# Restack from two queues, later staged splits, regrouped token work and later query parts in a two-layer cross-attention kernel

## The chip, the cores and the metric

The kernel runs on one core of a Trainium2 chip. The metric is the device time of one execution in microseconds (us), lower is better. The engines are PE (matrix multiply; PEld is its weight load), DVE (vector), ACT (scalar), POOL (GpSimd) and SP (which here only issues transfers). Each engine works through its own list of instructions in order and waits on semaphores.

## The reference

Two layers over queries x (8 batches of 64 rows, width 256) and a context of 8 x 1601 rows:

```
x = x + cross_attention_0(layernorm(x), ctx)      # 16 heads of width 16
x = x + head_attention(layernorm(x))
x = x + top1_expert_ffn(layernorm(x))             # 8 experts
x = x + cross_attention_1(layernorm(x), ctx)
x = x + state_space(layernorm(x))                 # 64-step scan, gelu, layer norm
x = x + top2_moe(layernorm(x))                    # router, gate/up/down with 8 experts
```

Everything is float32. The kernel writes many operands as two float16 parts, a high part and a low part, and makes three products of them (high x high, high x low, low x high).

## The kernel before

**Rounds and steps.** The two cross-attentions are 16 rounds `g` (8 batches in layer 0, then 8 in layer 1). The 1601 context rows are 13 row tiles, so each round has 13 steps `k`. `STEP_UNITS` writes out by hand what each step holds: `S` scores and their exponentials on ACT, `W` the weighted sum over values, `K`/`N` key projections of a later round in four quarters times two halves, `V` value projections, `P` score maxima (PE makes them, DVE reduces them into `mpart`), `T` and `O` the row constants and the division. A key unit K is made by PE, evacuated twice by ACT (`k32` at L1093, `kh` at L1094), and its low part `kl` is made by POOL (L643).

**Restacking.** `restack(r, mt)` on SP (L497) waits for the low parts of four key units and then issues 12 transfers that copy `kh` and `kl` into `ks`, the layout that the scores read. In round `g` SP does `restack(g + 1, 0)` in step 1 and `restack(g + 1, 1)` in step 8. Within a step SP's order is: restack, `load_high_queries`, context loads, and then the events of the step. Two things wait for `stacked0`: the scores of the round, and ACT's evacuation of the next round's first key units (L1088), since `kh` is reused. Before round 0 there is a prologue written out in `PROLOGUE_UNITS`.

**Events.** `MID` and `SSM` place the other work in the steps: key `n` of `MID` for token tile `t` falls on step 13 x (2t + 2) + 6 + n, counted from the start of round 0. The queries of layer 1 are made by `q_make` (PE, ACT), `q_parts`, `q_mask` and `q_store` (DVE), and SP's `store_queries` writes them to memory with three transfers that raise `q_out` by 48. Key 27 of tile t is step 7 of round 2t + 4. The head attention of tile t + 1 begins in the same round: its `a_v` falls on step 9, and DVE there waits for all earlier stores:

```
dve.wait_ge(sem("a_v_mm"), t + 1)
dve.wait_ge(sem("q_out"), 48 * (TT + t))
nc.vector.tensor_copy(a_v[:, :], mid[:, 0:D]).then_inc(sem("a_v"), 1)
```

PE's `a_qk` in step 10 writes the bank that this copy reads, so it waits for `a_v`. `STAGE_AT` places the splits of six staged weights (ACT makes the high part, DVE the low part), and SP loads a next one after each.

**The tail.** After round 15 `TAIL` lists by hand: `g` and `d` are parts of the gate product on PE; `x` scales and transposes tokens of one expert (POOL or ACT scales, PE transposes, ACT takes the high part) and `y` takes the low part on DVE; `h` and `l` are the high and low split of an expert weight tile (ACT, then DVE). `transpose_tokens(i)` waits for the low part of token group i - 2. Groups 26 to 39 stand among 32 `d` parts.

Of the kernel before, what the change touches and what calls it, by code (L numbers as in the profile page):

```python
# [13 lines left out]
P = 128  # L14
# [13 lines left out]
E = 8  # L28
# [25 lines left out]
PROLOGUE_UNITS = ("Q K0 K1 P0 P1 K2 P2 K3 P3 V0 P4 P5 K4 P6 P7 K5 P8 K6 P9 V1 P10 K7 P11 N0 P12 N1 P13 N2 P14 P15 "  # L54
                  "T N3").split()
FIRST_CTX_HIGH = {"K1": 4, "K3": 5, "V0": 6, "K4": 7}
FIRST_CTX_LOW = {"P2": 4, "P4": 5, "P6": 6, "P7": 7}
STEP_UNITS = {0: ["V2", "S", "P0", "W"],
              1: ["V3", "S", "P1", "W"],
# [23 lines left out]
MID = {0: ["out"], 1: ["a_norm"], 2: ["a_turn"], 3: ["a_v"], 4: ["a_qk"], 5: ["a_e"], 6: ["a_p"], 7: ["a_w"],  # L83
       8: ["a_z"], 9: ["a_x"], 10: ["f_norm"], 13: ["f_turn"], 14: ["f_gate"], 15: ["f_pick"], 16: ["f_0"],
       17: ["f_1"], 18: ["f_2"], 19: ["f_3"], 20: ["f_end"], 21: ["q_norm"], 22: ["q_turn"], 23: ["q_make"],
       24: ["q_parts"], 26: ["q_mask"], 27: ["q_store"]}

SSM = {0: ["out"], 1: ["s_norm"], 2: ["s_turn"], 3: ["s_u"], 4: ["s_0"], 5: ["s_1"], 6: ["s_2"], 7: ["s_3"],
       8: ["s_4"], 9: ["s_5"], 10: ["s_y"], 13: ["g_stats"], 14: ["g_norm"], 16: ["g_parts"], 17: ["g_clean"],
       18: ["m_stats"], 20: ["m_norm"], 21: ["m_turn"], 23: ["r_logits"], 27: ["r_pick"]}  # L90
SSM_THIRD = {0: ["out"], 1: ["s_norm"], 2: ["s_turn"], 3: ["s_u"], 4: ["s_0"], 5: ["s_1"], 6: ["s_2"], 7: ["s_3"],
             8: ["s_4"], 9: ["s_5"], 10: ["s_y"], 11: ["g_stats"], 12: ["g_norm"], 13: ["g_parts", "g_clean"],
             14: ["m_stats"], 15: ["m_norm"], 16: ["m_turn"], 17: ["r_logits"], 18: ["r_pick"]}
QUERIES = ["q_stats", "q_norm", "q_turn", "q_make", "q_parts", "q_mask", "q_store"]
FIRST = {(0, 0): 1, (1, 4): 2, (1, 9): 3}
STAGE_JOBS = 7
STAGE_AT = {(0, 2): 1, (0, 6): 2, (0, 8): 3, (0, 10): 4, (0, 12): 5, (1, 1): 6}
POWERS_AT = {(0, 7): 0, (0, 9): 1, (0, 11): 2, (0, 12): 3, (1, 0): 4}
SPLIT_AT = {(G - 1, 8): 0, (G - 1, 11): 1}

# [17 lines left out]
for e in range(E):  # L118
    TAIL += ["g"] * min(2, len(GATE_PARTS) - TAIL.count("g")) + [f"x{X_THIRD + e}", f"y{X_THIRD + e}"]
TAIL += ["g"] * (len(GATE_PARTS) - TAIL.count("g"))  # L120
for n in range(len(LAST_GATE_PARTS)):
    TAIL.append("d")
    if n % 2 and 0 <= (n - 3) // 2 < len(X) - X_BOTH:
        TAIL += [f"x{X_BOTH + (n - 3) // 2}", f"y{X_BOTH + (n - 3) // 2}"]
    if n % E == E - 1:
        TAIL += [f"h{GATES + n // E}", f"l{GATES + n // E}"]

UNITS = [(0, it) for it in range(GATES)] + [(1, it) for it in range(GATES)] + \
        [(r, it) for it in range(GATES, IT) for r in range(2)]
# [142 lines left out]
def build(nc, d, out):  # L272
    with ExitStack() as ctx:
# [10 lines left out]
        def need(eng, name, value):  # L284

            if value > 0:
                eng.wait_ge(sem(name), value)
# [179 lines left out]
        def _(sp):  # L467
# [29 lines left out]
            def restack(r, mt):  # L497

                sp.wait_ge(sem("klo_done"), K_UNITS * r + 4 * mt + 4)
                need(sp, "main_mm", 2 * KT * (r - 1) if r > 1 else 0)  # L500
                for j in range(4):
                    for n, part in enumerate((kh, kl, kh)):
                        load(ks[r % 2][n + 1:P:PARTS, 4 * mt + j, :], part[32 * j:32 * j + 32, mt, :], f"stacked{mt}")

# [125 lines left out]
        @block.gpsimd  # L630
        def _(pool):
            def load(dst, src, name):
                pool.dma_start(dst, src).then_inc(sem(name), 16)

            def inverse_root(i):

                pool.wait_ge(sem("var_ready"), i + 1)
                nc.gpsimd.tensor_tensor(rstd[:, :], ve[:, :], half[:, :], ALU.pow).then_inc(sem("rstd_ready"), 1)

            def klo(r, ku):  # L640
                mt, (k0, w) = ku // 4, QUARTERS[ku % 4]
                pool.wait_ge(sem("khi_done"), K_UNITS * r + ku + 1)
                nc.gpsimd.tensor_tensor(kl[:, mt, k0:k0 + w], k32[:, ku % 2, 0:w], kh[:, mt, k0:k0 + w],  # L643
                                        ALU.subtract).then_inc(sem("klo_done"), 1)

            def scale_tokens(i):

                r, e, t0, t1 = X[i]
                if i == 0:
                    pool.wait_ge(sem("k_mm"), K_UNITS * B)  # L650
                    pool.wait_ge(sem("v_mm"), V_UNITS * B)
                pool.wait_ge(sem("cmb_done"), t1)
                need(pool, "xcT_mm", i - 1)
                for t in range(t0, t1):
                    ins = nc.gpsimd.tensor_scalar(xg[:, i % 2, t - t0, :], xm[:, t, :], cmb[:, TT * r + t, e:e + 1], None,
                                                  ALU.mult)
                ins.then_inc(sem(f"xg_ready{i % 2}"), 1)

            def event(name, layer, t):
                if name == "r_pick" and t in (1, TT - 1):  # L660
                    for i in range(2):
                        scale_tokens((0 if t == 1 else X_THIRD) + i)
                elif name == "x":
                    if t + 2 < len(X) and t + 2 not in (X_THIRD, X_THIRD + 1) and not scaled_by_act(t + 2):
                        scale_tokens(t + 2)
                elif name == "q_stats":
                    inverse_root(t)
                elif name in ("out", "a_x", "f_end", "g_stats", "m_stats"):
                    to = {"out": "s_" if layer else "a_", "a_x": "f_", "f_end": "q_", "g_stats": "g_",
                          "m_stats": "m_"}[name]  # L670
                    inverse_root(stats_index(to, 1, t))

            nc.gpsimd.memset(half[:, :], -0.5).then_inc(sem("half_ready"), 1)
            nc.gpsimd.memset(qcur[0][:, :, :], 0.0)
            nc.gpsimd.memset(qcur[1][:, :, :], 0.0).then_inc(sem("qcur_zero"), 1)
            load(small[:, :], d["small"], "const_in")
            load(bias[:, :, :], d["bias"], "const_in")
            load(rows[:, :, :], d["rows"][:, 0:4, :], "const_in")
            load(sel[:, :], d["sel"], "const_in")
            load(fb32[:, :], d["fb"], "const_in")  # L680
            load(wo[:, :, :], d["wo"][0], "wo0_in")
            load(am[:, 0, :, :], d["am"], "am_in")
            load(bT[:, :, :], d["bT"], "ssm_in")
            load(cT[:, :], d["cT"], "ssm_in")
            load(rw[:, :, :, :], d["rw"], "rw_in")
            load(rdw[:, :, :], d["rdw"], "rw_in")
            pool.wait_ge(sem("half_ready"), 1)
            inverse_root(0)
            nc.gpsimd.memset(v[:, :, :, DH:VW], 1.0).then_inc(sem("v_ones"), 1)
            for ku in range(8):  # L690
                klo(0, ku)
            for ku in range(4):
                klo(1, ku)
            for g in range(G):
                for k in range(KT):
                    for name in STEP_UNITS[k]:
                        if name[0] in "KN" and has_unit(name, g):
                            klo(round_of(name, g), int(name[1]))
                    for name, layer, t in events(g, k):
                        event(name, layer, t)  # L700
            for item in TAIL:
                if item[0] == "x":
                    event("x", 1, int(item[1:]))
                else:
                    event(item, 1, TT - 1)
            for it in range(IT):
                pool.wait_ge(sem("ihi_done"), it + 1)
                nc.gpsimd.tensor_tensor(il[:, it, :], i32[:, it % 2, :], ih[:, it, :],
                                        ALU.subtract).then_inc(sem("ilo_done"), 1)
# [343 lines left out]
        def _(act):  # L1053
            def split_stage(z):
# [11 lines left out]
                    ins = nc.scalar.activation(fbp[:, 0, :], fb32[:, :], ACT.Copy, scale=W_SCALE)  # L1066
                ins.then_inc(sem("stage_hi"), 1)

            def split_ctx(n):
                g, i, s = n // 4, n % 4, ctx_slot(n)  # L1070
                h, kc, u = i // 2, i % 2, g % 2
                k0, w = HALVES[h]
                act.wait_ge(sem(f"ctx_in{s}"), 16 * ctx_loads(n))

                need(act, "v_mm", V_UNITS * (g - 2) + (4 if h == 0 else V_UNITS))
                need(act, f"parts_stored{u}", 32 * (g // 2))
                nc.scalar.activation(ch[u][:, kc, k0:k0 + w], c32[s][:, 0:w], ACT.Copy).then_inc(sem("chi_done"), 1)  # L1077
# [78 lines left out]
            def event(name, layer, t):  # L1156
# [8 lines left out]
                elif name == "q_make":  # L1165
# [3 lines left out]
                    for mt in range(2):  # L1169
# [3 lines left out]
                        else:  # L1173
                            ins = nc.scalar.activation(q32[:, mt, :], o, ACT.Copy)
                    ins.then_inc(sem("q32_done"), 1)
                elif name == "stage":
                    split_stage(t)
                elif name == "power":
# [58 lines left out]
            for name in PROLOGUE_UNITS:  # L1237
                if name != "Q":
                    after_unit(name, int(name[0] == "N"), True)
                if name in FIRST_CTX_HIGH:  # L1240
                    split_ctx(FIRST_CTX_HIGH[name])
            act.wait_ge(sem("const_in"), 80)
            for g in range(G):
                for k in range(KT):
# [42 lines left out]
        def _(dve):  # L1287
# [143 lines left out]
            def event(name, layer, t):  # L1431
# [72 lines left out]
                    stats(xt)  # L1504
                elif name == "q_parts":
                    q = TT * layer + t
                    dve.wait_ge(sem("q32_done"), q + 1)
                    need(dve, "q_out", 48 * q)
                    link(nc.vector.tensor_copy(qh[:, :, :], q32[:, :, :]))
                    link(nc.vector.tensor_tensor(ql[:, :, :], q32[:, :, :], qh[:, :, :], ALU.subtract))  # L1510
                elif name in ("q_mask", "q_store"):
                    two = range(2) if name == "q_mask" else range(2, 4)
# [205 lines left out]
```

## Time and profile before

| what | value |
|---|---|
| runs, median (lowest to highest) | 1031.73 us (1030.37 to 1033.67), 3 runs |
| the profiled execution | 1028.6 us, span 1026.8 us |
| mean granted clock of PE | 0.990 of full speed |
| PE, DVE, ACT, POOL busy | 92%, 60%, 53%, 20% |
| prologue before the first scores | 0 to 49.26 us |
| 16 rounds | 49.26 to about 735 us |
| tail and expert products | from about 735 us to the end |

Rows of a timeline read: start, duration, engine and line, operation, tiles, count; in square brackets the idle time of the engine just before it and what ended it. SPq is SP issuing a transfer. A waiting row of PE is time lost only where PE sets the end.

### The profile page before, as it was taken

What the parts mean: (1) busy time and instruction counts of PE and PEld (TensorE: products, weight loads), DVE (VectorE), ACT (ScalarE), POOL (GpSimd) and SP (SyncE); (2) the same over time, 40 slices, a digit from 0 to 9 for tenths busy, and PEclk for the clock granted to TensorE, in tenths of its full rate; (3) what the DMA queues carried; (4) which work ended last, traced back from release to release, by engine and by line L of the source; (5) the groups of instructions that cost most, each with busy time, mean ns of one, the idle gap of its engine ahead of it and who ended that gap; (6) DMA issues with size and microseconds to landing.
All of it is one profiled execution on the core that took longest, in us unless ns stands there. A gap on an engine that the chain in (4) does not pass through costs nothing.

```text
span 1026.8 us, 35579 instructions
## 1 busy us (share of the span) xinstructions
PE 947.6 (92%) x15476; PEld 625.1 (61%) x15476; DVE 620.9 (60%) x1046; ACT 545.0 (53%) x1032; POOL 201.2 (20%) x233
## 2 busy tenths in 40 slices
PE   4789889999999999999999999997898899999998
PEld 2356566656656665666666656656687544445887
DVE  5665665667485565857667776775764574445332
ACT  4467766776677667456666666656625421212200
POOL 4211112111111212111121121232446100000000
PEclk9999999999999999999999999999999999999999
DMA  8587375452735352454334444423221322232100
GB/s 301 137 313 231 87 253 133 143 169 73 209 92 156 107 129 70 116 133 122 93 113 119 107 120 119 103 56 126 85 83 41 124 101 104 82 107 99 42 1 22
DMA packets 70829, 123.79 MB, mean 121 GB/s; under 512 B 34770, under 2 KB 46082, under 8 KB 67412
## 3 DMA queue, kind: packets, MB, share of 16 engines
q1 hardware_dynamic: 69812, 119.84, 39.4%
q8 instruction: 124, 2.03, 0.8%
q0 software_dynamic: 576, 1.35, 0.4%
q10 hardware_dynamic: 288, 0.33, 0.1%
q14 instruction: 29, 0.24, 0.1%
HBM read 64.81 MB, written 17.32 MB: 80 GB/s over the span
## 4 chain that ended last, share of the span: by engine, by line
PE 72%; DVE 11%; ACT 7%; issue 4%; DMA 2%; SPq 2%; POOL 1%; ACTq 0%; DVEq 0%; POOLq 0%
PE ps L714 70%; DVE mpart L1354 3%; ACT p L1119 3%; SPq L469 2%; DVE rinv L1371 1%; DMA c32a<-in_ctxT 1%; ACT ch L1077 1%; DMA c32b<-in_ctxT 1%; PE ps L853 1%; DVE cl L1329 1%; ACT kh L1094 1%; DVE wl L1385 1%; ACT k L1093 1%; PE ps L883 1%; ACT wh L1134 1%
## 5 line engine op out<-in xcount | busy, mean ns | idle before, releaser
L1354 DVE TENSOR_REDUCE mpart<-ps 128x2 f32<-128x800 f32 (+1 forms) x256 | 252.5, 988 | 136.0 <-PE ps L714 135.1
L1119 ACT ACTIVATE p<-ps 128x512 f32<-128x512 f32 (+1 forms) x416 | 225.6, 595 | 186.2 <-PE ps L714 184.8
L643 POOL TENSOR_TENSOR kl<-k,kh 128x400 f16<-128x400 f32 (+1 forms) x128 | 117.6, 920 | 458.4 <-ACT kh L1094 458.4
L714 PE MATMUL ps<-p,v 128*17 128x64 f32 x6656 | 131.8, 222 | 1.6 <-issue 1.6
L714 PEld LDWEIGHTS ps<-p,v 128*17 128x17 f32 x6656 | 98.1, 98 | 39.8 <-issue 37.3
L714 PE MATMUL ps<-wvh,ch 128*128 128x256 f16 (+1 forms) x416 | 114.3, 275 | 1.9 <-issue 1.9
L714 PE MATMUL ps<-xch,wh 128*128 128x512 f16 (+2 forms) x384 | 114.3, 312 | 0.0
L714 PE MATMUL ps<-xcl,wh 128*128 128x512 f16 (+2 forms) x384 | 114.2, 311 | 0.0
L714 PE MATMUL ps<-xch,wl 128*128 128x512 f16 (+2 forms) x384 | 114.0, 311 | 0.0
L714 PE MATMUL ps<-wvl,ch 128*128 128x256 f16 (+1 forms) x416 | 113.5, 273 | 0.0
L714 PE MATMUL ps<-wvh,cl 128*128 128x256 f16 (+1 forms) x416 | 113.4, 273 | 0.0
L714 PE MATMUL ps<-kh,qbcur 64*128 64x400 f16 (+1 forms) x512 | 86.8, 336 | 25.4 <-DVE mpart L1354 22.1
L1385 DVE SCALAR_TENSOR_TENSOR wl<-w,wh 128x2048 f16<-128x2048 f32 x24 | 55.0, 2291 | 82.9 <-ACT wh L1134 82.9
L714 PEld LDWEIGHTS ps<-qcur,ks 64*128 64x128 f16 (+1 forms) x3328 | 61.3, 97 | 65.5 <-issue 51.3
L714 PE MATMUL ps<-qcur,ks 64*128 64x64 f16 (+1 forms) x3328 | 85.7, 192 | 10.5 <-ACT p L1119 6.1
L714 PE MATMUL ps<-ch,wkh 128*128 128x400 f16 (+1 forms) x256 | 87.7, 342 | 7.7 <-ACT kh L1094 6.0
L714 PE MATMUL ps<-ch,wkl 128*128 128x400 f16 (+1 forms) x256 | 86.9, 339 | 0.0
L714 PE MATMUL ps<-cl,wkh 128*128 128x400 f16 (+1 forms) x256 | 86.7, 339 | 0.0
L1134 ACT ACTIVATE wh<-w 128x2048 f16<-128x2048 f32 x24 | 45.7, 1903 | 64.4 <-PE ps L714 64.4
L714 PE MATMUL ps<-wh,ih 128*128 128x256 f16 x256 | 69.8, 273 | 0.0
L714 PE MATMUL ps<-wl,ih 128*128 128x256 f16 x256 | 69.8, 273 | 0.0
L714 PE MATMUL ps<-wh,il 128*128 128x256 f16 x256 | 69.8, 273 | 0.0
(207 smaller groups left out, 1452.8 us busy)
## 6 DMA issues: line engine op xcount, KB each, us to landing
ks<-kh SPq DMA_DIRECT2D x256, 100.1 KB
w<-in_wgu SPq DMA_DIRECT2D x16, 1024.0 KB, 4.9
ks<-kl SPq DMA_DIRECT2D x128, 100.1 KB
w<-in_wd SPq DMA_DIRECT2D x8, 1024.0 KB, 4.7
c32a<-in_ctxT SPq DMA_DIRECT2D x16, 400.5 KB, 5.0
cparts<-ch SPq DMA_DIRECT2D x8, 800.5 KB, 6.6
cparts<-cl SPq DMA_DIRECT2D x8, 800.5 KB, 8.8
c32a<-in_ctxT SPq DMA_DIRECT2D x12, 400.0 KB, 3.2
```

What stands on the lines that cost most here:

```text
L469: sp.dma_start(dst, src).then_inc(sem(name), 16)
L643: nc.gpsimd.tensor_tensor(kl[:, mt, k0:k0 + w], k32[:, ku % 2, 0:w], kh[:, mt, k0:k0 + w], ALU.subtract).then_inc(sem("klo_done"), 1)
L714: return nc.tensor.matmul(o, lhsT, rhs, start=start, stop=stop, skip_group_check=shared)
L853: last = nc.tensor.transpose(o, xg[:, i % 2, t, P * kc:P * kc + P], ident[:, :])
L883: last = nc.tensor.transpose(mid[:, P * kc:P * kc + P], src[:, P * kc:P * kc + P], ident[:, :])
L1077: nc.scalar.activation(ch[u][:, kc, k0:k0 + w], c32[s][:, 0:w], ACT.Copy).then_inc(sem("chi_done"), 1)
L1093: nc.scalar.activation(k32[:, i % 2, 0:w], o[:, 0:w], func, **how).then_inc(sem("k32_done"), 1)
L1094: nc.scalar.activation(kh[:, mt, k0:k0 + w], o[:, 0:w], func, **how).then_inc(sem("khi_done"), 1)
L1119: nc.scalar.activation(p32[0:n, step % PRING, BANK * side:BANK * side + BANK], ps[0:n, side, :], ACT.Exp, scale=DH ** -0.5).then_inc(sem(" ...
L1134: nc.scalar.activation(wh[:, w % W_RING, :], w32[:, w % 3, :], ACT.Copy, scale=W_SCALE)\
L1354: nc.vector.reduce_max(mpart[:, j0:j0 + 3:2, quarter], o.rearrange("p (b c) -> p b c", b=2)[:, :, 0:w], AX.X).then_inc(sem("max_done"), 1)
L1385: nc.vector.scalar_tensor_tensor(wl[:, w % W_RING, :], w32[:, w % 3, :], W_SCALE, wh[:, w % W_RING, :], ALU.mult, ALU.subtract).then_inc(s ...
```

## The change

- The two restacks before round 0 are split: SP issues six of the 12 transfers, ACT the other six. ACT does so after evacuating K5 (first half) and N0 (second half).
- In the prologue POOL computes the first inverse root ahead of six loads that it issues, instead of behind them.
- The query high part `qh` is made by ACT right after `q32`, and not by DVE in `q_parts`. ACT waits there for the earlier query stores.
- `MID`: `q_parts`, `q_mask`, `q_store` move from keys 24, 26, 27 to 26, 27, 28. Key 28 is step 8 of round 2t + 4.
- `SSM`: `g_norm`, `g_parts`, `g_clean`, `m_stats` move from 14, 16, 17, 18 to 16, 17, 18, 19, and `r_pick` from 27 to 30.
- `STAGE_AT`: the six staged splits come one or two steps later.
- `TAIL`: token groups 26 to 30 stand one pair of `d` parts earlier. The split of weight tile 4 (`h4 l4`) follows the tenth `d` part instead of the eighth, with six `d` parts behind it. Token groups 31 to 38 stand one pair later, group 39 one part later, and the splits of weight tiles 5, 6 and 7, which stood behind the parts 16, 24 and 32, all follow the last `d` part.

```diff
@@ -54,6 +54,7 @@
 PROLOGUE_UNITS = ("Q K0 K1 P0 P1 K2 P2 K3 P3 V0 P4 P5 K4 P6 P7 K5 P8 K6 P9 V1 P10 K7 P11 N0 P12 N1 P13 N2 P14 P15 "
                   "T N3").split()
 FIRST_CTX_HIGH = {"K1": 4, "K3": 5, "V0": 6, "K4": 7}
+FIRST_RESTACK = {"K5": 0, "N0": 1}
 FIRST_CTX_LOW = {"P2": 4, "P4": 5, "P6": 6, "P7": 7}
 STEP_UNITS = {0: ["V2", "S", "P0", "W"],
               1: ["V3", "S", "P1", "W"],
@@ -83,18 +84,18 @@
 MID = {0: ["out"], 1: ["a_norm"], 2: ["a_turn"], 3: ["a_v"], 4: ["a_qk"], 5: ["a_e"], 6: ["a_p"], 7: ["a_w"],
        8: ["a_z"], 9: ["a_x"], 10: ["f_norm"], 13: ["f_turn"], 14: ["f_gate"], 15: ["f_pick"], 16: ["f_0"],
        17: ["f_1"], 18: ["f_2"], 19: ["f_3"], 20: ["f_end"], 21: ["q_norm"], 22: ["q_turn"], 23: ["q_make"],
-       24: ["q_parts"], 26: ["q_mask"], 27: ["q_store"]}
+       26: ["q_parts"], 27: ["q_mask"], 28: ["q_store"]}
 
 SSM = {0: ["out"], 1: ["s_norm"], 2: ["s_turn"], 3: ["s_u"], 4: ["s_0"], 5: ["s_1"], 6: ["s_2"], 7: ["s_3"],
-       8: ["s_4"], 9: ["s_5"], 10: ["s_y"], 13: ["g_stats"], 14: ["g_norm"], 16: ["g_parts"], 17: ["g_clean"],
-       18: ["m_stats"], 20: ["m_norm"], 21: ["m_turn"], 23: ["r_logits"], 27: ["r_pick"]}
+       8: ["s_4"], 9: ["s_5"], 10: ["s_y"], 13: ["g_stats"], 16: ["g_norm"], 17: ["g_parts"], 18: ["g_clean"],
+       19: ["m_stats"], 20: ["m_norm"], 21: ["m_turn"], 23: ["r_logits"], 30: ["r_pick"]}
 SSM_THIRD = {0: ["out"], 1: ["s_norm"], 2: ["s_turn"], 3: ["s_u"], 4: ["s_0"], 5: ["s_1"], 6: ["s_2"], 7: ["s_3"],
              8: ["s_4"], 9: ["s_5"], 10: ["s_y"], 11: ["g_stats"], 12: ["g_norm"], 13: ["g_parts", "g_clean"],
              14: ["m_stats"], 15: ["m_norm"], 16: ["m_turn"], 17: ["r_logits"], 18: ["r_pick"]}
 QUERIES = ["q_stats", "q_norm", "q_turn", "q_make", "q_parts", "q_mask", "q_store"]
 FIRST = {(0, 0): 1, (1, 4): 2, (1, 9): 3}
 STAGE_JOBS = 7
-STAGE_AT = {(0, 2): 1, (0, 6): 2, (0, 8): 3, (0, 10): 4, (0, 12): 5, (1, 1): 6}
+STAGE_AT = {(0, 4): 1, (0, 7): 2, (0, 9): 3, (0, 11): 4, (1, 0): 5, (1, 2): 6}
 POWERS_AT = {(0, 7): 0, (0, 9): 1, (0, 11): 2, (0, 12): 3, (1, 0): 4}
 SPLIT_AT = {(G - 1, 8): 0, (G - 1, 11): 1}
 
@@ -118,12 +119,15 @@
 for e in range(E):
     TAIL += ["g"] * min(2, len(GATE_PARTS) - TAIL.count("g")) + [f"x{X_THIRD + e}", f"y{X_THIRD + e}"]
 TAIL += ["g"] * (len(GATE_PARTS) - TAIL.count("g"))
+TOKENS_AT = dict(zip((1, 3, 5, 7, 9, 15, 17, 19, 21, 23, 25, 27, 29, 30), range(X_BOTH, len(X))))
 for n in range(len(LAST_GATE_PARTS)):
     TAIL.append("d")
-    if n % 2 and 0 <= (n - 3) // 2 < len(X) - X_BOTH:
-        TAIL += [f"x{X_BOTH + (n - 3) // 2}", f"y{X_BOTH + (n - 3) // 2}"]
-    if n % E == E - 1:
-        TAIL += [f"h{GATES + n // E}", f"l{GATES + n // E}"]
+    if n in TOKENS_AT:
+        TAIL += [f"x{TOKENS_AT[n]}", f"y{TOKENS_AT[n]}"]
+    if n == 9:
+        TAIL += [f"h{GATES}", f"l{GATES}"]
+for w in range(GATES + 1, 2 * GATES):
+    TAIL += [f"h{w}", f"l{w}"]
 
 UNITS = [(0, it) for it in range(GATES)] + [(1, it) for it in range(GATES)] + \
         [(r, it) for it in range(GATES, IT) for r in range(2)]
@@ -498,7 +502,7 @@
 
                 sp.wait_ge(sem("klo_done"), K_UNITS * r + 4 * mt + 4)
                 need(sp, "main_mm", 2 * KT * (r - 1) if r > 1 else 0)
-                for j in range(4):
+                for j in range(4 if r else 2):
                     for n, part in enumerate((kh, kl, kh)):
                         load(ks[r % 2][n + 1:P:PARTS, 4 * mt + j, :], part[32 * j:32 * j + 32, mt, :], f"stacked{mt}")
 
@@ -678,14 +682,14 @@
             load(rows[:, :, :], d["rows"][:, 0:4, :], "const_in")
             load(sel[:, :], d["sel"], "const_in")
             load(fb32[:, :], d["fb"], "const_in")
+            pool.wait_ge(sem("half_ready"), 1)
+            inverse_root(0)
             load(wo[:, :, :], d["wo"][0], "wo0_in")
             load(am[:, 0, :, :], d["am"], "am_in")
             load(bT[:, :, :], d["bT"], "ssm_in")
             load(cT[:, :], d["cT"], "ssm_in")
             load(rw[:, :, :, :], d["rw"], "rw_in")
             load(rdw[:, :, :], d["rdw"], "rw_in")
-            pool.wait_ge(sem("half_ready"), 1)
-            inverse_root(0)
             nc.gpsimd.memset(v[:, :, :, DH:VW], 1.0).then_inc(sem("v_ones"), 1)
             for ku in range(8):
                 klo(0, ku)
@@ -1066,6 +1070,14 @@
                     ins = nc.scalar.activation(fbp[:, 0, :], fb32[:, :], ACT.Copy, scale=W_SCALE)
                 ins.then_inc(sem("stage_hi"), 1)
 
+            def restack_first(mt):
+
+                act.wait_ge(sem("klo_done"), 4 * mt + 4)
+                for j in range(2, 4):
+                    for n, part in enumerate((kh, kl, kh)):
+                        act.dma_start(ks[0][n + 1:P:PARTS, 4 * mt + j, :], part[32 * j:32 * j + 32, mt, :])\
+                           .then_inc(sem(f"stacked{mt}"), 16)
+
             def split_ctx(n):
                 g, i, s = n // 4, n % 4, ctx_slot(n)
                 h, kc, u = i // 2, i % 2, g % 2
@@ -1173,6 +1185,9 @@
                         else:
                             ins = nc.scalar.activation(q32[:, mt, :], o, ACT.Copy)
                     ins.then_inc(sem("q32_done"), 1)
+                    act.wait_ge(sem("q32_done"), q + 1)
+                    need(act, "q_out", 48 * q)
+                    nc.scalar.activation(qh[:, :, :], q32[:, :, :], ACT.Copy).then_inc(sem("qh_done"), 1)
                 elif name == "stage":
                     split_stage(t)
                 elif name == "power":
@@ -1239,6 +1254,8 @@
                     after_unit(name, int(name[0] == "N"), True)
                 if name in FIRST_CTX_HIGH:
                     split_ctx(FIRST_CTX_HIGH[name])
+                if name in FIRST_RESTACK:
+                    restack_first(FIRST_RESTACK[name])
             act.wait_ge(sem("const_in"), 80)
             for g in range(G):
                 for k in range(KT):
@@ -1504,9 +1521,8 @@
                     stats(xt)
                 elif name == "q_parts":
                     q = TT * layer + t
-                    dve.wait_ge(sem("q32_done"), q + 1)
+                    dve.wait_ge(sem("qh_done"), q + 1)
                     need(dve, "q_out", 48 * q)
-                    link(nc.vector.tensor_copy(qh[:, :, :], q32[:, :, :]))
                     link(nc.vector.tensor_tensor(ql[:, :, :], q32[:, :, :], qh[:, :, :], ALU.subtract))
                 elif name in ("q_mask", "q_store"):
                     two = range(2) if name == "q_mask" else range(2, 4)
```

## Rows read from the trace of the kernel before

**Rows 1.** The page, its first part: busy time, share of span, instructions.

```profile
PE 947.6 (92%) x15476; PEld 625.1 (61%) x15476; DVE 620.9 (60%) x1046; ACT 545.0 (53%) x1032; POOL 201.2 (20%) x233
```

**Rows 2.** Timeline of SP in round 4 (steps 7 to 9): query stores, restack, loads.

```profile
254.87 0.38 SPq L469 DMA_DIRECT2D qscratch<-qh  x1
...
255.80 0.47 SPq L469 DMA_DIRECT2D qbscratch<-qb  x1
256.37 0.50 SPq L469 DMA_DIRECT2D ks<-kh  x1
...
265.00 0.47 SPq L469 DMA_DIRECT2D c32a<-in_ctxT  x1
```

**Rows 3.** Timeline of SP in rounds 6 and 8: restack's first issue, and `qbcur` behind it.

```profile
347.00 0.50 SPq L469 DMA_DIRECT2D ks<-kh  x1
...
357.30 0.53 SPq L469 DMA_DIRECT2D qbcur<-qbscratch  x1
...
435.48 0.50 SPq L469 DMA_DIRECT2D ks<-kh  x1
...
445.55 0.52 SPq L469 DMA_DIRECT2D qbcur<-qbscratch  x1
```

**Rows 4.** Timeline of POOL, the last `kl` that each of these restacks waits for.

```profile
252.72 0.89 POOL L643 TENSOR_TENSOR kl<-k,kh 128x400 f16<-128x400 f32 x1 [1.22 <-ACT kh L1094]
...
345.92 0.89 POOL L643 TENSOR_TENSOR kl<-k,kh 128x400 f16<-128x400 f32 x1 [1.46 <-ACT kh L1094]
...
434.56 0.89 POOL L643 TENSOR_TENSOR kl<-k,kh 128x400 f16<-128x400 f32 x1 [1.63 <-ACT kh L1094]
```

**Rows 5.** Timeline of PE, `a_qk` of tiles 1, 2 and 3.

```profile
263.01 1.98 PE L714 MATMUL ps<-aw,xnT 128*128 128x512 f32 x4 [0.34 <-DVE a_v L1454]
...
354.36 1.98 PE L714 MATMUL ps<-aw,xnT 128*128 128x512 f32 x4
...
442.83 1.98 PE L714 MATMUL ps<-aw,xnT 128*128 128x512 f32 x4
```

**Rows 6.** Timeline of DVE, the copy that waits for the stores.

```profile
262.54 0.41 DVE L1454 COPY a_v<-ps 128x256 f32<-128x256 f32 x1
```

**Rows 7.** The tile `qbscratch`, all its transfers: issue to landing.

```profile
DMA to landing us min/median/max: 2.5/2.9/6.8
```

**Rows 8.** Windows: stretch, length, engines busy, PEclk (granted clock), DMA share, GB/s.

```profile
40.00:42.00 2.00, 2.00 (x6) 0.66 (x6) 0.00 (x0) 0.69 (x2) 1.82 (x2) 0.50 0.51 104
...
788.00:792.00 4.00, 4.00 (x39) 3.87 (x38) 1.38 (x2) 2.74 (x5) 1.61 (x3) 0.63 0.60 240
...
804.00:808.00 4.00, 4.00 (x22) 1.89 (x20) 1.73 (x2) 2.99 (x3) 0.00 (x0) 0.57 0.62 246
```

**Rows 9.** Timelines of SP and PE in the prologue.

```profile
28.34 0.61 SPq L469 DMA_DIRECT2D ks<-kh  x1
28.99 0.59 SPq L469 DMA_DIRECT2D ks<-kl  x1
...
39.95 0.50 PE L714 MATMUL ps<-ch,wkh 128*128 128x400 f16 x1 [2.54 <-ACT kh L1094]
...
49.26 0.41 PE L714 MATMUL ps<-qcur,ks 64*128 64x64 f16 x16 [1.11 <-DMA ks<-kh]
```

**Rows 10.** Timeline of PE: the first key product, and a maximum late in round 0.

```profile
12.70 0.49 PE L714 MATMUL ps<-ch,wkh 128*128 128x401 f16 x1 [0.23 <-DVE cl L1329]
...
66.90 0.34 PE L714 MATMUL ps<-kh,qbcur 64*128 64x400 f16 x2 [1.22 <-DVE mpart L1354]
```

**Rows 11.** Timeline of PE after `g_norm` in round 11.

```profile
566.09 0.34 PE L714 MATMUL ps<-kh,qbcur 64*128 64x400 f16 x2 [0.88 <-DVE mpart L1354]
```

**Rows 12.** PE's waits from 770 to 800 us (total, times, longest), then timelines of DVE and PE.

```profile
PE ps L853 <- DVE xcl L1393: 4.3, 2, 2.1
...
784.41 2.29 DVE L1385 SCALAR_TENSOR_TENSOR wl<-w,wh 128x2048 f16<-128x2048 f32 x1 [1.11 <-ACT wh L1134]
...
803.53 0.63 PE L853 MATMUL ps<-ident,xg 128*128 128x128 f32 x4 [2.30 <-DVE xcl L1393]
```

## The prediction

> **What bounds the kernel now.** I read the page first: PE is busy for 92% of the span and no other engine for more than 60% [rows 1]. So a microsecond matters where PE stands idle, or where it works at the lower clock. I then asked for PE's idle stretches (the brackets of its timeline) and, for each moved step, for the timelines of the engines that issue it and wait for it. Three places came out: the prologue, where transfers that SP issues one by one hold up PE [rows 9]; the tail, where PE waits for low parts that stand behind weight splits on DVE [rows 12]; and round 4, 6 and 8, where PE hardly waits today, but where the moved query store meets a waiting instruction [rows 2 to 6]. The third decides this forecast.
>
> **The query store, one step later.** Today SP stores the layer-1 queries of tile t in step 7, ahead of restack (the store's first row at 254.87, restack's first at 256.37) [rows 2]. With key 28 the store is an event of step 8. SP goes through its list in order, and there `restack(g + 1, 1)` with its 12 issues stands first, then `qbcur`, then in round 4 one context load. DVE's `a_v` copy in step 9 waits for that store to have landed. Behind it on DVE stand all later maxima, and PE's `a_qk` in step 10 waits for the copy. So one step less in the table costs about 10 us on SP's queue.
>
> How late is it? Restack can begin when the last `kl` is done: 252.72 + 0.89 = 253.61, 346.81 and 435.45 us [rows 4]. PE reaches `a_qk` at 263.01, 354.36 and 442.83 [rows 5]. That leaves 9.4, 7.55 and 7.4 us. What has to fit in there:
> - restack and the loads behind it, as SP issues them now: 256.37 to 265.47 = 9.1 us in round 4 [rows 2], 347.00 to 357.83 = 10.8 us in round 6, 435.48 to 446.07 = 10.6 us in round 8 [rows 3];
> - the store's first two issues, 254.87 to 255.80 = 0.9 us [rows 2];
> - the landing of the third transfer, median 2.9 us after its issue [rows 7];
> - the copy itself, 0.41 us [rows 6].
>
> Together 13.3, 15.0 and 14.8 us, so PE waits 3.9, 7.5 and 7.4 us longer: **+18.8 us**. None of it is hidden: PE's whole list stands behind `a_qk`. The bounds: 12 issues at the prologue's spacing of 0.65 us (28.34 to 28.99) [rows 9] are 7.8 us, and with `qbcur` 0.55, the store 0.9, the shortest landing 2.5 and the copy 0.4 that is 12.2 (12.7 in round 4), which gives 3.3 + 4.6 + 4.8 = 12.7 us. The longest landing, 6.8 us [rows 7], adds 3.9 to each wait, 30.5 in all. I take the median landing, since the queue is loaded at that place as it is for most of the other stores, and keep 12.7 and 30.5 for the range. Tile 3's store has no `a_v` behind it, and costs nothing: nothing reads it for two rounds.
>
> **The clock after these waits.** After 2.54 us of idleness at 39.95 [rows 9] the granted clock was 0.50, the 1.2 GHz level, from 40 to 42 [rows 8]. After the waits in the tail the window 788 to 792 was granted 0.63 and 804 to 808 0.57: 4 x 0.37 = 1.5 and 4 x 0.43 = 1.7 us of work lost. Three longer waits at 1.6 us each: **+4.8 us**. Bounds 0 and 6.
>
> **Two queues for the first restack.** SP needs 28.34 to about 36 us for its 12 issues, and ACT's evacuation of N0 waits for their landing, PE 2.54 us for that; the scores wait another 1.11 us [rows 9]. With six issues SP is done some 3.9 us earlier (6 x 0.65). ACT pays 3.9 us twice, which keeps the evacuations of K6 and of N1 waiting: K7 follows late on PE, about 2 us, in exchange for the wait before N2. Followed unit by unit I get the first scores 1.3 to 2.8 us earlier. SP's later loads are 4 to 5 us earlier too, which should take most of the 1.22 us at 66.90 [rows 10]. I book **-3.5 us**, with bounds -6 and +2 (ACT's 7.8 us of issues exposed, less what is saved).
> In that stretch the transfer engines are half busy (share 0.51 at 40 to 42 us) [rows 8], so it is the issuing that is slow. The Trainium skill, "DMA: Bandwidth & Descriptors", section "Issuing engines are not separate DMA queues", says that transfers issued from several engines interleave on the same 16 DMA engines, and its rules add that this saves only issue time. Were the transfers themselves the limit, this part would give 0 instead of 3.5 and the total would be 3.5 us higher; with a share of one half the trace speaks for the gain.
>
> **The tail.** Three waits of PE for low parts, 4.3 + 2.30 = 6.6 us [rows 12], each come from an `h l` pair among the tokens (the low split alone is 2.29 us on DVE). One pair stays in, now with six `d` parts beside it where there were two; the four more are some 0.6 us of cover that counts, so its wait of 2.2 us becomes 1.6, 5.0 us go, and about 1 us is given back where POOL's scaling becomes the pace. The clock no longer falls, 1.5 + 1.7 us [rows 8]. **-7 us**, bounds -3 and -9. The three splits that now stand last take about 3 x 2.3 = 6.9 us of DVE, beside a unit of 48 products which PE runs without them; if that cover were gone it would cost up to 3 us.
>
> **Small parts.** `g_norm` in step 7 delays the maxima of step 8, 0.88 us of PE at 566.09 [rows 11], and the same again in round 13; its later place gives **-2 us** (bounds -4 and +1, if it delays step 9 instead). `qh` on ACT and `q_parts` out of step 4: -0.3. The inverse root is some 2.3 us earlier, but PE's first key product waits for a context low part and not for it, 0.23 us at 12.70 [rows 10]: 0. Staged splits and `r_pick`: 0, as their readers come rounds later; where they now fall they take about 2 us of ACT and DVE each, and without slack there they would cost up to 1 us apiece, 4 in all.
>
> **Sum.** 18.8 + 4.8 - 3.5 - 7 - 2 - 0.3 = +10.8 us. The profiled span 1026.8 becomes 1037.6, its execution 1028.6 becomes 1039.4, and since the median of the runs lies 3.1 us above that execution, the median becomes 1042.5. I say **1042 us**.
>
> **Rivals.**
> - *The store is in time* (faster). Then only the gains are left: -12.8 us, 1019 us. For this, restack, loads, store and landing would have to fit into 7.4 us; the landing and the copy alone take 3.3, so SP would have to make its 16 issues in 4 us. Every restack in the trace speaks against it. It decides from the point where a restack's 12 issues take under 3 us. Chance 0.08.
> - *The waits are there but short, and the gains full.* Clean issues, shortest landings, no fall of the clock: +12.7 less gains of up to 13 to 15: 1029 to 1033, no difference to be measured. Chance 0.07.
> - *The store is late and the prologue loses too.* ACT's issues stop the evacuations for 7.8 us and the staged splits cost 4 us: +18.8 + 4.8 + 2 + 4 - 9 = +21, 1052 us. Chance 0.15; longer landings lead there too.
> - *The forecast*: 0.70.
>
> **How the numbers follow.** A difference under 0.3% (3.1 us) can't be told from none here. Faster: 0.08 for the first rival and 0.02 for short waits. Same: 0.05. Slower: 0.85. The range leaves out the first rival and the ends of the bounds: low end +12.7 with a little clock loss (2) less 13 = +1.7, 1033; high end 1053. The forecast case alone lies between 1037 and 1047.
>
> **What would show it.** After the change PE's timeline has a wait before `a_qk` of tiles 1, 2 and 3, ended by DVE `a_v`, of about 4, 7.5 and 7.5 us, and none before that of tile 0. On SP the `qscratch` rows of rounds 4, 6 and 8 stand behind the 12 `ks` rows. The granted clock after each wait is near 0.5 for some 3 us. The first scores start at 46.5 to 48 us, and among the token groups of the tail one wait for a low part is left of three, below 2 us. The prediction is wrong if the `a_v` waits are under 2 us, or if the rounds between them change by more than 1 us each.

## Result and the profile after

The change makes the kernel slower: 1045.38 us (median of 5, 1040.02 to 1046.06) against 1031.60 us before (1028.49 to 1033.67); the ratio is 1.0141, 95% interval 1.0112 to 1.017. Forecast were 1042 us and slower by more than 0.3%. The profiled execution after took 1040.02 us with a span of 1038.2 us, against 1028.6 and 1026.8. It is the fastest of its five runs, so its 11.4 us of longer span are 2.4 us fewer than the medians differ (13.8).

The page after, first part, answers to [rows 1]: busier by 4 us in PE, with the same work.

```profile
PE 951.7 (92%) x15476; PEld 626.6 (60%) x15476; DVE 618.2 (60%) x1038; ACT 549.2 (53%) x1040; POOL 197.8 (19%) x233
```

Timeline of PE after, `a_qk` of tiles 0 to 3, answers to [rows 5]:

```profile
174.24 1.98 PE L718 MATMUL ps<-aw,xnT 128*128 128x512 f32 x4 [0.34 <-DVE a_v L1471]
...
269.60 3.78 PE L718 MATMUL ps<-aw,xnT 128*128 128x512 f32 x4 [5.34 <-DVE a_v L1471]
...
367.46 3.78 PE L718 MATMUL ps<-aw,xnT 128*128 128x512 f32 x4 [6.40 <-DVE a_v L1471]
...
463.64 3.51 PE L718 MATMUL ps<-aw,xnT 128*128 128x512 f32 x4 [6.59 <-DVE a_v L1471]
```

Tile 0, which waits for no layer-1 store, waits as before. The other three wait 18.3 us together where they waited 0.3. The product behind each wait also takes 3.5 to 3.8 us instead of 1.98: it runs at half clock. The windows say the same (columns as in [rows 8]):

```profile
270.00:272.00 2.00, 2.00 (x3) 0.77 (x3) 0.44 (x1) 0.00 (x0) 0.00 (x0) 0.50 0.45 47
272.00:274.00 2.00, 2.00 (x5) 0.61 (x4) 0.00 (x0) 0.50 (x1) 0.00 (x0) 0.50 0.90 215
...
368.00:370.00 2.00, 2.00 (x3) 0.67 (x2) 0.30 (x1) 0.00 (x0) 0.00 (x0) 0.50 0.50 53
...
464.00:466.00 2.00, 2.00 (x3) 0.81 (x3) 0.49 (x1) 0.00 (x0) 0.00 (x0) 0.50 0.45 51
```

The fall lasts longest behind tile 1, where 274 to 276 is still at 0.60; behind tiles 2 and 3 the next windows are at 0.71 and 0.81. By these windows I estimate that the three falls took 3.0, 1.85 and 1.55 us of PE's work, 6.4 us in all.

Timeline of SP in round 4, answers to [rows 2]: restack first, the store behind it.

```profile
255.22 0.50 SPq L473 DMA_DIRECT2D ks<-kh  x1
...
262.84 1.13 SPq L473 DMA_DIRECT2D qbcur<-qbscratch  x1
264.01 0.44 SPq L473 DMA_DIRECT2D c32a<-in_ctxT  x1
264.50 0.43 SPq L473 DMA_DIRECT2D qscratch<-qh  x1
264.97 0.47 SPq L473 DMA_DIRECT2D qscratch<-ql  x1
265.48 0.52 SPq L473 DMA_DIRECT2D qbscratch<-qb  x1
```

Timeline of DVE, the three copies, answers to [rows 6]; their idle time ends with the landing of exactly that transfer:

```profile
269.12 0.42 DVE L1471 COPY a_v<-ps 128x256 f32<-128x256 f32 x1 [4.91 <-DMA qbscratch<-qb]
...
366.98 0.43 DVE L1471 COPY a_v<-ps 128x256 f32<-128x256 f32 x1 [8.62 <-DMA qbscratch<-qb]
...
463.16 0.42 DVE L1471 COPY a_v<-ps 128x256 f32<-128x256 f32 x1 [8.80 <-DMA qbscratch<-qb]
```

**Where the time went.** The same instructions of PE serve as marks in both traces. They stand later by -0.2 us at the first scores (49.07 against 49.26), +2.4 at `a_qk` of tile 0, +6.6, +13.1 and +20.8 at tiles 1, 2 and 3, +19.3 at the `out` addition of round 14 (698.42 against 679.08), +19.5 at token group 26 (798.14 against 778.63) and +11.4 at the end. So three things happened: a loss of 2.6 us in rounds 0 to 2 that was not forecast, a loss of 18.4 us in rounds 2 to 8, and gains of 1.5 us up to round 14 and 8.1 us in the tail.

The loss of 18.4 us is smaller than its parts. Up to `a_qk` of tile 3 the waits are 18.0 us longer than before and the first two falls of the clock take 4.85 us, 22.9 in all, so 4.5 us came back in these rounds. Before, PE waited 7.8 us there for `mpart` and once 1.9 us for "issue"; after, it waited 5.4 us for `mpart` and not for "issue".

Timeline of PE in the tail, token groups 26, 33 and 39, answers to [rows 12]: one wait for a low part is left of three, 1.27 us long.

```profile
798.14 0.64 PE L857 MATMUL ps<-ident,xg 128*128 128x128 f32 x4
...
809.69 0.63 PE L857 MATMUL ps<-ident,xg 128*128 128x128 f32 x4 [1.27 <-DVE xcl L1410]
...
817.01 0.61 PE L857 MATMUL ps<-ident,xg 128*128 128x128 f32 x4
```

### The profile page after: what moved, and what is told of

It reads as the page before. It is cut to its first block, busy times and chain, and to the rows that moved or that the text cites. A ratio compares the mean times of both kernels' runs of the same rounds, so it can differ in the third digit from the quotient of the medians.

```text
span 1038.2 us, 35590 instructions
## 1 busy us (share of the span) xinstructions
PE 951.7 (92%) x15476; PEld 626.6 (60%) x15476; DVE 618.2 (60%) x1038; ACT 549.2 (53%) x1040; POOL 197.8 (19%) x233
## 4 chain that ended last, share of the span: by engine, by line
PE 72%; DVE 10%; ACT 7%; issue 4%; DMA 2%; SPq 2%; POOL 1%; ACTq 1%; DVEq 0%; POOLq 0%
PE ps L718 70%; DVE mpart L1371 3%; ACT p L1131 2%; SPq L473 2%; DVE rinv L1388 2%; DVE cl L1346 1%; PE ps L857 1%; ACT ch L1089 1%; POOL xg L659 1%; ACT kh L1106 1%; ACT k L1105 1%; DMA qbscratch<-qb 1%; DMA c32a<-in_ctxT 1%; DMA ks<-kh 1%; PE ps L887 1%
```

## Experiments

Ratios are to the kernel before on the same chip, with 95% intervals. Kernel names: "changed" is the kernel after the change.

**1. The changed kernel with the old query places.**

```diff
-       26: ["q_parts"], 27: ["q_mask"], 28: ["q_store"]}
+       24: ["q_parts"], 26: ["q_mask"], 27: ["q_store"]}
```

> The changed kernel with only the MID keys of q_parts, q_mask and q_store put back to 24, 26, 27. If the store behind restack on SP is the loss, the three waits before a_qk (5.3, 6.4, 6.6 us) go and with them about 1.7 us of half clock after each: 1045.4 - 18 - 5 = about 1022 us, faster than before. The rival, that the waits only gather time that is lost elsewhere anyway (DVE, restack, tail), expects 1035 us or more.

Measured: 1023.69 us, ratio 0.9946 (0.9915 to 0.9977), where the whole change has 1.0141. The waits before `a_qk` of tiles 1 to 3 are 0.34, 0 and 0 again, and the time is within 2 us of the 1022 expected. These three numbers in a table are worth 2.0% or 20 us, and without them the rest of the change is a gain of 5.6 us.

**2. The kernel before with the new query places alone.**

```diff
-       24: ["q_parts"], 26: ["q_mask"], 27: ["q_store"]}
+       26: ["q_parts"], 27: ["q_mask"], 28: ["q_store"]}
```

> The kernel before with only the three MID keys moved. If the store behind restack is the loss: three waits of 5 to 8 us before a_qk and 1.7 us of half clock after each, 1031.6 + 18 + 5 = about 1055 us. The rival, that the waits need another part of the change as well (qh on ACT, the moved splits): under 1040 us.

Measured: 1051.43 us (4 runs, 1046.86 to 1057.4), ratio 1.0245 (1.0205 to 1.0286), 25 us. The waits are 5.05, 7.05 and 6.26 us, each product behind them takes 3.78 us. Nothing else of the change is needed for the loss. Timeline of PE, tile 2:

```profile
364.38 3.78 PE L714 MATMUL ps<-aw,xnT 128*128 128x512 f32 x4 [7.05 <-DVE a_v L1454]
```

**3. The new places kept, but SP issues the store ahead of the restack of step 8.**

```diff
                     if k == 8 and g + 1 < G:
+                        for name, layer, t in events(g, k):
+                            if name == "q_store":
+                                event(name, layer, t)
                         restack(g + 1, 1)
```

(In the event loop further down the store of step 8 is then left out.)

> The changed kernel, keys 26, 27, 28 kept, but SP issues the query store of step 8 ahead of that step's restack. If SP's order makes the store late, it lands before or within 1 us of a_v: 1022 to 1027 us and a_v waits under 1.5 us each. The rival, that the store is late since DVE finishes its operands a step later and the landing takes its time, expects waits of 4 us or more and over 1038 us.

Measured: 1036.99 us, ratio 1.0078 (1.0048 to 1.0108), which lies between the two expectations. The waits for `a_v` are gone (0.34, 0 and 0), so SP's order was what made the store land late. But the time did not come down to that of experiment 1, which differs from this run only in the places and SP's order: of the 20 us between the changed kernel (1.0141) and experiment 1 (0.9946) only 6.5 are won back, a third. Timeline of SP from round 4 on:

```profile
263.94 0.38 SPq L473 DMA_DIRECT2D qscratch<-qh  x1
...
265.44 0.50 SPq L473 DMA_DIRECT2D ks<-kh  x1
...
275.31 1.36 SPq L473 DMA_DIRECT2D scratch<-a_v  x2
...
280.92 0.33 SPq L473 DMA_DIRECT2D a_w<-scratch  x1
```

And of PE, the products on the `a_w` of tiles 1 and 2, and for each the next product with the weights `aw` (1.13 us in the one, 2.08 us in the other):

```profile
283.13 0.66 PE L930 MATMUL ps<-ident,a_w 128*128 128x128 f32 x2 [2.78 <-issue]
...
287.57 1.13 PE L722 MATMUL ps<-aw,a_wT 128*128 128x256 f32 x4
...
376.17 0.66 PE L930 MATMUL ps<-ident,a_w 128*128 128x128 f32 x2 [2.92 <-issue]
...
381.39 2.08 PE L722 MATMUL ps<-aw,a_wT 128*128 128x256 f32 x4
```

The last `kl` for this restack is done at 259.63, but restack starts at 265.44, as SP now stands before it waiting for the store's operands, which DVE makes one step later than before. The `a_v` rows and the load of `a_w` behind it come late in turn, and PE waits 2.78, 2.92 and 3.81 us for `a_w`, once behind each of tiles 1 to 3. The row says "issue"; that PE waits for the load of `a_w` is argued and not shown by the row. For it speaks that the same product waited at most 0.3 us before, and that the loads are issued at 280.92, 373.16 and 469.96 and take 2.1 to 2.9 us to land in this trace, which is when PE goes on (283.13, 376.17, 472.11).

The granted clock makes these waits dear. Behind tile 1 it was at 0.50 from 284 to 286 and 0.87 up to 288, a loss of about 1.7 us. Behind tiles 2 and 3 it was at 0.50 up to 384 and 480, and at 0.62 and 0.73 in the next 2 us, a loss of about 4.7 and 4.5 us (estimates from windows of 2 us). With the waits of 9.5 us that makes 20.4 us; from `a_qk` of tile 1 to the end this trace is 15.9 us longer than that of experiment 1, and by the medians it is 13.3 us. So both theories hold a part: the order on SP makes the `a_v` wait, but with the store put first, its later operands hold up the restack and all behind it, and that costs two thirds of what the wait did. The moved splits (experiment 4) are in this run and in experiment 1 alike.

**4. The staged splits, alone and taken back.** The first run is the kernel before with only `STAGE_AT` moved; the second is the kernel of experiment 1 with `STAGE_AT` put back as well.

```diff
-STAGE_AT = {(0, 2): 1, (0, 6): 2, (0, 8): 3, (0, 10): 4, (0, 12): 5, (1, 1): 6}
+STAGE_AT = {(0, 4): 1, (0, 7): 2, (0, 9): 3, (0, 11): 4, (1, 0): 5, (1, 2): 6}
```

> The kernel before with only STAGE_AT moved. In the changed kernel's trace the maxima waited 1.8 us at 69.6 and 1.3 us at 81.6 where splits now stand, and from the first scores to the first a_qk it lost 2.6 us. If the moved splits are the cause, this run is 1.5 to 3 us slower than before, with a_qk of tile 0 at 173.5 to 175 us against 171.9. The rival, that the earlier loads or the saturated transfer engines are the cause, expects a_qk within 0.7 us of before.

> The changed kernel with the MID keys and STAGE_AT put back. If the moved splits cost 2 to 3 us, it is 2 to 3 us under the run with the MID keys alone put back (0.9946 of before), about 0.992; if they cost nothing, it stands at the same ratio.

Measured: alone 1034.63 us, ratio 1.0045 (1.0022 to 1.0068), 4.7 us; taken back 1020.83 us, ratio 0.992 (0.9895 to 0.9945), 2.7 us under experiment 1 though with overlapping intervals. The profiled execution of the first is the longest of its eleven (span 1039.0) and shows more than this part: its longest wait, 4.12 us at 67.92, follows a context load that landed at 65. The clean case stands in the trace of the changed kernel. Timeline of DVE in the changed kernel:

```profile
67.36 0.69 DVE L1330 SCALAR_TENSOR_TENSOR wkl<-stage,wkh 128x512 f16<-128x512 f32 x1 [1.57 <-ACT wvh L1065]
67.97 0.68 DVE L1330 SCALAR_TENSOR_TENSOR wvl<-stage,wvh 128x512 f16<-128x512 f32 x1
68.58 0.98 DVE L1371 TENSOR_REDUCE mpart<-ps 128x2 f32<-128x800 f32 x1
```

And of PE there, the scores whose PSUM buffer the maximum gives free:

```profile
69.62 0.34 PE L718 MATMUL ps<-kh,qbcur 64*128 64x400 f16 x2 [1.80 <-DVE mpart L1371]
...
81.58 0.34 PE L718 MATMUL ps<-kh,qbcur 64*128 64x400 f16 x2 [1.32 <-DVE mpart L1371]
```

DVE waits 1.57 us for ACT's high parts and then splits for 1.2 us, while a maximum that PE needs waits behind it.

One trace alone would not show this loss: in five kernels whose lists are the same up to there (before, experiment 2, and the three of experiment 6), `a_qk` of tile 0 stands between 171.1 and 174.5 us. Taken from the first scores on, all traces together speak more clearly. From there to `a_qk` of tile 0 the four kernels with the moved splits take 125.2 us (changed and experiment 3), 126.1 (experiment 1) and 131.6 (splits alone, the trace with the late context load). Of the nine with the old places eight take 118.9 to 122.9, and one, SSM alone, 125.3.

**5. The two-queue first restack, alone and with a hold.** The first run is the kernel before with `FIRST_RESTACK`, `restack_first` and the shortened loop. The second adds one line on SP:

```diff
+            sp.wait_ge(sem("stacked1"), 16 * 12)
             load(ks[1][0:P:PARTS, :, :], d["ones"], "ones_in1")
```

> The kernel before with only the two-queue first restack. First scores were at 49.26 us before and 49.07 with the whole change, though the last restack issue came 6 us earlier. Theory: ACT's six transfers land late since SP, now free earlier, puts 4 MB of large transfers beside them; then first scores at 48.5 to 49.5 us here too and the time within 2 us of before. The rival, that the two queues do bring what was forecast and another part of the change (inverse root, qh on ACT) takes it back: first scores at 46.5 to 48 us and 2 to 3.5 us faster.

> As the run with only the two-queue restack, and SP waits for the landing of the second half (stacked1) before it issues the constant rows and the stores of the parts. If the large transfers delay the small ones, the scores' wait for ks falls away and they start at 46 to 47.5 us, and the time is 1 to 3 us under the run without the hold, less what the later context loads cost. If the ks transfers are slow for another reason, first scores stay at 49 us and the time gets worse by the hold, 2 us or more.

Measured: ratio 0.9987 (0.9961 to 1.0012) and 0.9988 (0.9966 to 1.0011); neither can be told from none, nor from each other. Of the first expectation the time held (1.3 us faster, within 2) and the first scores came a little later than its 48.5 to 49.5, at 49.94. Of the second the wait for `ks` fell away as expected, but the first scores came at 49.02 and not at 46 to 47.5, and the time got no better. Timeline of SP in the changed kernel, its last restack issues:

```profile
40.67 0.60 SPq L473 DMA_DIRECT2D ks<-kh  x1
41.31 0.59 SPq L473 DMA_DIRECT2D ks<-in_ones  x1
```

Of ACT, its last one:

```profile
40.98 0.61 ACTq L1078 DMA_DIRECT2D ks<-kh  x1
```

And of PE, the first scores, which answers to [rows 9]:

```profile
49.07 0.41 PE L718 MATMUL ps<-qcur,ks 64*128 64x64 f16 x16 [1.72 <-DMA ks<-kh]
```

The last issue ends at 41.6 us, the last landing is at 49.0: 7.4 us. In between SP puts 4 MB of large transfers into the same engines. With the two-queue restack alone the same two times are 42.4 and 49.9, 7.5 us. With the hold, SP goes on at 44.89, which is when the 12 transfers have landed: 2.7 us after the last issue, ACT's, has ended (41.59 + 0.62). So the large transfers delay the small ones. Timelines of SP and PE in the run with the hold:

```profile
44.89 0.48 SPq L470 DMA_DIRECT2D ks<-in_ones  x1
...
44.42 0.76 PE L716 MATMUL ps<-ident,m 128*1 128x128 f16 x8 [2.74 <-DVE m L1375]
...
49.02 0.41 PE L716 MATMUL ps<-qcur,ks 64*128 64x64 f16 x16
```

The first scores come at 49.02 without a wait for `ks`: PE has key and value products and the slow clock in front of them, from `T` at 44.42 on. So in this run the transfers were not what set this point. In the changed kernel they still were, for the 1.72 us of the row above: there `T` stood at 42.63. What `T` waits for is the row maximum `m` of DVE, and no run here takes apart what sets that.

Nor is the forecast gain to be found anywhere else. In the seven traces with the two-queue restack the first scores start between 49.0 and 54.0 us, in the six without it between 48.7 and 49.8. Part of the lateness lies further ahead: in experiment 3, in experiment 7 and in the second run of experiment 4, products of score maxima between 17 and 26 us took 0.52 us instead of 0.35; why is open.

**6. The tail alone, SSM alone, both.** The kernel before with the new `TAIL`, with the new `SSM`, and with both.

> The kernel before with only the new TAIL. Expected from the traces: one wait for a low part of three is left and the clock stays at its upper level in the tail: 8 to 9 us faster, about 1023 us. The rival, that part of the tail's 8.8 us comes from where POOL and DVE stand when the tail begins: 5 us or less.

> The kernel before with only the SSM places moved. Forecast: -2 us, the waits of 0.9 us for mpart in rounds 11 and 13 gone and nothing new: span from a_qk of tile 3 to the 'out' event of round 14 shorter by 2 to 3 us than the 236 us of before. The rival, that the later steps pay for it: no shorter.

> The kernel before with the new TAIL and the new SSM places alone. From the traces: tail 7 to 8 us, SSM 2 to 3 us, together 9 to 11 us: 1020 us, ratio 0.990. If so, the two-queue restack, the inverse root and qh on ACT bring nothing that can be told (the run with all of them stood at 0.992). If these do help, this run stays above 0.994.

Measured: tail 0.996 (0.9936 to 0.9984), SSM 0.9979 (0.9957 to 1.0), both 0.9919 (0.9894 to 0.9944). From token group 26 to the end six kernels with the new tail (the changed one, the two of this section, experiments 1 and 7 and the second of 4) took 240.0 to 240.1 us, five with the old tail (before, both of experiment 5, SSM alone, the splits alone) 245.9 to 248.2. So the tail is worth 6 to 8 us in the traces. Its timed 4.1 us is less than the 8 to 9 expected and has an interval of 1.6 to 6.6; the two meet only near 6 us. In the SSM run the wait of 0.88 us at [rows 11] is gone, and from `a_qk` of tile 3 to `out` of round 14 it took 233.9 us, 2.3 us less than before.

**7. Everything that helps.** The changed kernel with the old query places, the old `STAGE_AT` and the hold.

> The changed kernel with MID keys and STAGE_AT put back and SP's hold behind the first restack. The run without the hold stood at 0.992 of before. If the hold is worth nothing over a whole execution, as the restack runs say, the ratio is 0.990 to 0.993, about 1021 us. The rival, that the earlier first scores (1.6 us at a_qk of tile 0) are kept to the end: 0.990 or less.

Measured: 1019.35 us, ratio 0.9913 (0.9879 to 0.9946), the fastest kernel here, but not to be told from tail and SSM alone (0.9919). The restack from two queues, the earlier inverse root and `qh` on ACT bring nothing that these runs can show. The rival, that earlier first scores are kept to the end, found nothing to keep: here they start at 50.62, without a wait for `ks`.

## Why the prediction was right, point by point

- **The query store.** The mechanism and the size held: forecast +18.8 us of waiting, measured 18.3 less the 0.3 of before. The split was off: 3.9, 7.5 and 7.4 forecast, 5.0, 6.4 and 6.6 found. From restack's first issue to the store's third SP took 10.3, 11.0 and 10.2 us where 10.0, 11.7 and 11.5 were forecast: in round 4 `qbcur` took 1.13 us to issue, and in rounds 6 and 8 the slow issues of [rows 3] were fewer, restack to `qbcur` taking 8.6 us in round 8 against 10.1 before. The landings took 3.6, 2.6 and 3.4 us, forecast 2.9. That figure mixes the stores into `qbscratch` with the loads out of it [rows 7]; before, the stores alone had a median of 3.4 us and the loads 2.8. Experiments 1, 2 and 3 show the cause: places in the table, alone enough, through SP's order.
- **The clock.** Forecast 3 x 1.6 us. The product right behind each wait is longer by 1.8, 1.8 and 1.5 us alone, and the windows give 6.4 us, a little above the bound of 6. The waits and the clock together make 24.4 us, forecast 23.6, where experiments 1 and 2 measure 20 and 25. "None of it is hidden" was too strong: up to tile 3 4.5 us came back, and in the rounds between tiles 1 and 2 alone 2.9 (the marks lie 6.5 us further apart, with 6.4 of wait and 3.0 of clock). That is more than the 1 us per round that was named as a sign of being wrong.
- **Two queues for the first restack.** Forecast -3.5, measured -1.3 with an interval of -4 to +1.2. The step that failed is the price of issuing: a shorter list on SP was taken for earlier landings, and the landings for what sets the first scores. SP's last issue came 6 us earlier, and the first scores, forecast at 46.5 to 48 us, came at 49.07 against 49.26. Of this stretch the trace showed a transfer share of one half [rows 8], and I set the rule of the Trainium skill, "DMA: Bandwidth & Descriptors", section "Issuing engines are not separate DMA queues", aside for that. By that rule, all transfers share the same 16 engines, and the trace after agrees: once SP is early, its large transfers are early too, and the last small one took 7.4 us. The share was read in the kernel in which they did not yet overlap.
- **Staged splits.** Booked at 0 with up to 4 us if there were no slack; measured +4.7 alone and +2.7 in company. The failed step is "readers come rounds later": that says nothing of who stands behind the split on ACT and DVE, and those were the maxima.
- **Tail.** Forecast -7, with one wait of 1.6 us left; found -8.1 in the trace (against the longest of the old tails; -4.1 timed alone), 1.27 us left, and no fall of the clock.
- **SSM.** Forecast -2; measured -2.2 (0 to -4.4).
- **The sum.** The runs form a chain. Everything but the query places and the moved splits (experiment 4's second run) is 8.2 us faster than the kernel before; the moved splits add 2.7 us to it, and the query places 20.1. That these make +14.6, as measured, holds by construction. Set against the forecast they show that its nearness (+10.8) is in part luck. The query store and its clock cost 3.5 us less than the 23.6 booked; the moved splits cost 2.7 where 0 was booked; the restack, the inverse root and `qh` brought nothing where 3.8 was booked (0.992 with them, 0.9919 without); tail and SSM brought 8.3 of 9. One error of 3.5 us stands against three of 7.3 us together. Counted from the side of the kernel before, the parts make 25.2 + 4.7 - 8.3 - 1.3 = 20.3, which is 6 us too many. The intervals of the parts (about 4, 2.4, 2.6 and 2.6 us) allow most of it; whether parts also cover each other stays open.

## What to carry to other kernels

When an event moves by one step, read the queue that issues it and not the step length: here one step of about 3.4 us moved three small transfers behind twelve others, and an engine that waits for their landing stood still for 5 to 9 us, three times. A transfer's place has two neighbours, and mending the order alone passed most of the lateness on to the next one behind (experiment 3). And a queue that gets through its list sooner also starts the large transfers behind it sooner.

## What was not expected of the hardware

- The length of a wait did not say what it cost in clock. After waits of 5.34, 6.40 and 6.59 us the granted clock was at 0.50, the 1.2 GHz level, for about 6, 4 and 3 us of work, a loss of 3.0, 1.85 and 1.55 us. After waits of 2.78, 2.92 and 3.81 us in experiment 3 it stayed there for about 3, 9 and 9 us, a loss of 1.7, 4.7 and 4.5, and after 2.54 us in the prologue of the kernel before the loss was 1.7 (0.50 from 40 to 42, 0.64 from 42 to 44).
- Twelve transfers of 100 KB that had landed 2.7 us after the end of their last issue when alone took 7.4 us beside 4 MB in large ones (experiment 5).
- The part of the kernel behind token group 26 repeated to within 0.1 us over six kernels with the same tail, while `a_qk` of tile 0 stood at 171.1 to 174.5 us in five kernels with the same list up to there. A gain of 2 us there can't be told from a single profile.
